# Attention's P times V as two overlapping 128-column products instead of a main product and paired 64-column tails

## What is computed

```python
def _L0_attn_ref(x, W_qkv, b_qkv, W_proj, b_proj):
    b, n, c = x.shape                       # 16, 128, 192
    q, k, v = jnp.split(x @ W_qkv + b_qkv, 3, axis=-1)
    q = q.reshape(b, 8, n, 192)             # likewise k and v
    energy = jnp.einsum('bhqd,bhkd->bhqk', q, k)
    attn = jax.nn.softmax(energy, axis=-1) / 192 ** 0.5
    out = jnp.einsum('bhal,bhlv->bhav', attn, v)
    return out.reshape(b, n, 8 * 192) @ W_proj + b_proj
```

## Time and profile before

| | us |
|---|---|
| median of 3 runs (940.44, 940.95, 943.34) | 940.95 |
| the profiled execution | 939.32 |
| its span, first to last instruction | 937.6 |
| PE busy in the span | 816.1 |
| DVE busy | 526.9 |
| ACT busy | 487.3 |
| attention's P times V, first to last start | 77.8 to 423.6 |
| the next block's first matmul | 433.51 |

### The profile page before, as it was taken

The page is one execution under the profiler, slowest core; times in us unless marked ns, Lnnn a source line. Parts: engine busy times, 40 slices in busy tenths (PEclk is TensorE's granted clock), DMA queues, the critical chain, the costliest instruction groups (busy, mean ns, idle before and its releaser), DMA issues. The chain is left out here.

```text
span 937.6 us, 16696 instructions
## 1 busy us (share of the span) xinstructions
PE 816.1 (87%) x6264; PEld 725.3 (77%) x6264; DVE 526.9 (56%) x1388; ACT 487.3 (52%) x1298; POOL 192.2 (20%) x285
## 2 busy tenths in 40 slices
PE   0599999999999999985685868669989999999997
PEld 0488999999999998974564646558878888898887
DVE  5763645454545454345666656525877556566564
ACT  2255454545353535331566757845645665576653
POOL 4561010202020202021002211200115106042070
PEclk9899999999999999997689989999999999999999
DMA  8433333333333333333001101230000000000000
GB/s 236 115 80 69 77 69 77 69 76 69 77 68 77 69 77 68 77 69 88 1 2 59 61 19 43 60 90 1 1 1 1 1 18 1 1 18 1 17 1 19
DMA packets 33617, 47.34 MB, mean 50 GB/s; under 512 B 4672, under 2 KB 28608, under 8 KB 33536
## 3 DMA queue, kind: packets, MB, share of 16 engines
q1 hardware_dynamic: 28240, 34.63, 16.1%
q0 software_dynamic: 2544, 9.05, 3.4%
q10 hardware_dynamic: 2752, 2.59, 1.1%
HBM read 30.53 MB, written 15.73 MB: 49 GB/s over the span
## 5 line engine op out<-in xcount | busy, mean ns | idle before, releaser
L1488 DVE TENSOR_TENSOR ffn_hid_lo<-ffn_gelu,ffn_hid_hi 128x512 fp32r<-128x512 f32 x120 | 98.0, 818 | 107.2 <-ACT ffn_hid_hi L1462 106.2
L1416 PE MATMUL ffn_ps_out<-ffn_weights_w,ffn_hid_hi 128*128 128x384 f32 x480 | 144.8, 358 | 3.5 <-DVE ffn_hid_lo L1488 3.3
L1458 ACT ACTIVATE ffn_gelu<-ffn_ring,ffn_b 128x512 f32<-128x512 f32 x120 | 82.3, 686 | 113.3 <-PE ffn_ring L1405 111.0
L1417 PE MATMUL ffn_ps_out<-ffn_weights_w,ffn_hid_lo 128*128 128x192 f32 x480 | 121.1, 252 | 0.0
L450 POOL TENSOR_SCALAR attn_probs<-attn_probs,attn_inverse 128x128 f32<-128x128 f32 x128 | 48.2, 376 | 297.2 <-DVE attn_inverse L738 289.5
L1416 PEld LDWEIGHTS ffn_ps_out<-ffn_weights_w,ffn_hid_hi 128*128 128x128 f32 x480 | 90.5, 189 | 9.8 <-DVE ffn_hid_lo L1488 4.9
L1417 PEld LDWEIGHTS ffn_ps_out<-ffn_weights_w,ffn_hid_lo 128*128 128x128 f32 x480 | 91.8, 191 | 4.2
L607 ACT ACTIVATE attn_probs<-ps_scores,attn_neg_max 128x128 f32<-128x128 f32 x128 | 45.3, 366 | 77.6 <-DVE attn_neg_max L734 77.6
L1462 ACT ACTIVATE ffn_hid_hi<-ffn_gelu 128x512 fp32r<-128x512 f32 x120 | 75.9, 633 | 3.8
L1047 ACT ACTIVATE mix_probs<-mix_ps_scores,mix_neg_max 128x128 f32<-128x128 f32 x192 | 67.4, 392 | 17.5 <-DVE mix_neg_max L1145 17.5
L1346 POOL TENSOR_SCALAR ffn_bias_part<-ffn_b,ffn_gates 128x192 f32<-128x192 f32 x64 | 37.4, 600 | 135.8 <-DVE ffn_gates L1522 134.7
(11 more groups left out here) (272 smaller groups left out, 2152.6 us busy)
## 6 DMA issues: line engine op xcount, KB each, us to landing
v_rows<-attn_v_flat SPq DMA_DIRECT2D x16, 768.0 KB, 3.3
attn_v_rows<-v_rows SPq DMA_DIRECT2D x128, 96.0 KB, 3.7
mix_stage<-in_w POOLq DMA_DIRECT2D x5, 576.0 KB, 5.7
mix_stage<-in_w POOLq DMA_DIRECT2D x10, 192.0 KB, 3.4
mix_stage<-in_w POOLq DMA_DIRECT2D x5, 384.0 KB, 4.4
attn_stage_main<-in_w_qkv SPq DMA_DIRECT2D x2, 768.0 KB, 9.0
h_rows<-hin SPq DMA_DIRECT2D x8, 192.0 KB, 2.8
ffn_base<-h_rows SPq DMA_DIRECT2D x1, 1536.0 KB, 9.6
```

Source lines behind the costliest of these rows:

```text
L1416: nc.tensor.matmul(ps_out[:, b, 0:2 * D], hid_hi[:, i % 3, tile], w2[:, c, :, :], start=c == 0, stop=False)
L1417: last = nc.tensor.matmul(ps_out[:, b, 0:D], hid_lo[:, i % 3, tile], w2[:, c, 0, :], start=False, stop=c == HC - 1)
L1458: nc.scalar.activation(gelu[:, i % 2, :], ring[:, bank("L1", i), :], ACT.Gelu, bias=b1[:, f * HC + c:f * HC + c + 1]).then_inc(chunk_read, 1)
L1488: nc.vector.tensor_tensor(hid_lo[:, i % 3, :], gelu[:, i % 2, :], raw(hid_hi[:, i % 3, :]), ALU.subtract).then_inc(lo_ready, 1)
```

## The change

M computes two full products per group: V's dimensions 0 to 127 (side 0) and 64 to 191 (side 1), each 128 columns of weights and 128 streamed columns. Both sides lie in `ps_mixed`, which now has two banks; `ps_pairs` is gone. Dimensions 64 to 127 are computed twice. For even chunks R takes dimensions 64 to 191 from side 1 as a full slice and dimensions 0 to 63 from side 0 on partitions 0 to 63; for odd chunks it takes dimensions 0 to 127 from side 0 and dimensions 128 to 191 from side 1 on partitions 64 to 127. So `mixed_rows` again has twelve slices, eight with one chunk and four with two chunks, and no data changes partition. ACT does side 1 (`take_uppers`: 128x256 and 64x256), DVE side 0 (`take_lowers`: 128x256 and 64x256). The rows of the output weights are laid out accordingly on the host.

```diff
-        ps_mixed = ps("ps_mixed", [P, QUAD, P])
-        ps_pairs = ps("ps_pairs", [P, 512])
+        ps_mixed = ps("ps_mixed", [P, 2, QUAD, P])
...
                 for j, g in enumerate(groups):
-                    nc.tensor.matmul(ps_mixed[:, j, :], v_rows[:, b, g, 0:MAIN], pt[:, n % 2, j, :], start=True, stop=True)
-                for j, g in enumerate(groups):
-                    by_side = pt[:, n % 2, j, :].rearrange("p (c o t) -> p o c t", o=2, t=GROUP)
-                    for odd in range(2):
-                        out = pairs_of(slice(odd * TAIL, (odd + 1) * TAIL))[:, j, :].rearrange("p (c t) -> p c t", t=GROUP)
-                        last = nc.tensor.matmul(out, v_rows[:, b, g, MAIN:D], by_side[:, odd], start=True, stop=True)
+                    for side, cols in enumerate((slice(0, MAIN), slice(TAIL, D))):
+                        last = nc.tensor.matmul(ps_mixed[:, side, j, :], v_rows[:, b, g, cols], pt[:, n % 2, j, :], start=True, stop=True)
                 last.then_inc(mixed.sem, 1)
...
-        def o_place(n, tails):
-
-            at, kinds = (n % (QUADS // UNIT)) * QUAD * GROUP, slice(CHUNKS, KTILES) if tails else slice(0, CHUNKS)
-            return mixed_rows[:, kinds, at:at + QUAD * GROUP].rearrange("p c (j t) -> p j c t", t=GROUP)
+        def o_place(n, part, kinds):
+
+            at = (n % (QUADS // UNIT)) * QUAD * GROUP
+            return mixed_rows[part, kinds, at:at + QUAD * GROUP].rearrange("p c (j t) -> p j c t", t=GROUP)
...
+        def from_mixed(part, side, odd):
+            return ps_mixed[part, side, :, :].rearrange("p j (c o t) -> p j o c t", o=2, t=GROUP)[:, :, odd]
...
-                nc.scalar.activation(o_place(n, False), from_mixed(False), ACT.Copy).then_inc(mains_taken.sem, 1)
+                for part, kinds, odd in ((slice(0, P), slice(0, PAIRS), 0), (slice(TAIL, P), slice(CHUNKS, KTILES), 1)):
+                    last = nc.scalar.activation(o_place(n, part, kinds), from_mixed(part, 1, odd), ACT.Copy)
+                last.then_inc(uppers_taken.sem, 1)
...
-                nc.vector.tensor_copy(o_place(n, True), from_mixed(True)).then_inc(tails_taken.sem, 1)
+                for part, kinds, odd in ((slice(0, P), slice(PAIRS, CHUNKS), 1), (slice(0, TAIL), slice(CHUNKS, KTILES), 0)):
+                    last = nc.vector.tensor_copy(o_place(n, part, kinds), from_mixed(part, 0, odd))
+                last.then_inc(lowers_taken.sem, 1)
...
+    w_even, w_odd = w_proj[0::2], w_proj[1::2]
...
-        "w_proj_main": w_proj[:, :MAIN].transpose(1, 0, 2).reshape(MAIN, QKV),
-        "w_proj_tail": w_proj[:, MAIN:].reshape(CHUNKS // 2, P, D).transpose(1, 0, 2).reshape(P, QKV // 2),
+        "w_proj_main": np.concatenate([w_even[:, TAIL:], w_odd[:, :MAIN]]).transpose(1, 0, 2).reshape(MAIN, QKV),
+        "w_proj_tail": np.concatenate([w_even[:, :TAIL], w_odd[:, MAIN:]], axis=1).transpose(1, 0, 2).reshape(P, QKV // 2),
```

More of the change, by code:

```diff
@@ L307, in attention @@
         mixed = Signal(sem("mixed"), QUADS, lent=QUADS)
-        mains_taken = Signal(sem("mains_taken"), QUADS, lent=1)
-        tails_taken = Signal(sem("tails_taken"), QUADS, lent=1)
+        uppers_taken = Signal(sem("uppers_taken"), QUADS, lent=1)
+        lowers_taken = Signal(sem("lowers_taken"), QUADS, lent=1)
         out_filled = Signal(sem("out_filled"), UNIT, lent=1)
@@ L456, in attention @@
         out_of = lambda b: ps_scores[:, b, :, :].rearrange("p j k -> p (j k)")[:, 0:D]
-        pairs_of = lambda part: ps_pairs[part, 0:QUAD * PAIRS * GROUP].rearrange("p (j k) -> p j k", j=QUAD)
         @block.tensor
@@ L527, in mix @@
                 wait_emptied(pe, turn, source)
-                pe.wait_ge(mains_taken.sem, mains_taken.at(turn, n - 1))
+                pe.wait_ge(uppers_taken.sem, uppers_taken.at(turn, n - 1))
                 apart(pe, keep["passed"])
-                pe.wait_ge(tails_taken.sem, tails_taken.at(turn, n - 1))
+                pe.wait_ge(lowers_taken.sem, lowers_taken.at(turn, n - 1))
                 groups = range(n * QUAD - b * GROUPS, (n + 1) * QUAD - b * GROUPS)
                 for j, g in enumerate(groups):
-                    nc.tensor.matmul(ps_mixed[:, j, :], v_rows[:, b, g, 0:MAIN], pt[:, n % 2, j, :], start=True, stop=True)
-                for j, g in enumerate(groups):
-                    by_side = pt[:, n % 2, j, :].rearrange("p (c o t) -> p o c t", o=2, t=GROUP)
-                    for odd in range(2):
-                        out = pairs_of(slice(odd * TAIL, (odd + 1) * TAIL))[:, j, :].rearrange("p (c t) -> p c t", t=GROUP)
-                        last = nc.tensor.matmul(out, v_rows[:, b, g, MAIN:D], by_side[:, odd], start=True, stop=True)
+                    for side, cols in enumerate((slice(0, MAIN), slice(TAIL, D))):
+                        last = nc.tensor.matmul(ps_mixed[:, side, j, :], v_rows[:, b, g, cols], pt[:, n % 2, j, :], start=True, stop=True)
                 last.then_inc(mixed.sem, 1)
@@ L544, in project_out @@
                 if part == 0:
-                    pe.wait_ge(mains_taken.sem, mains_taken.at(turn, (b + 1) * (QUADS // UNIT) - 1))
-                    pe.wait_ge(tails_taken.sem, tails_taken.at(turn, (b + 1) * (QUADS // UNIT) - 1))
+                    pe.wait_ge(uppers_taken.sem, uppers_taken.at(turn, (b + 1) * (QUADS // UNIT) - 1))
+                    pe.wait_ge(lowers_taken.sem, lowers_taken.at(turn, (b + 1) * (QUADS // UNIT) - 1))
                     if b == 0:
@@ L565, in from_ring @@
             return ring[part, bank(slot), 0:UT].rearrange("p (g t) -> p g t", t=GROUP)
-        def o_place(n, tails):
-            at, kinds = (n % (QUADS // UNIT)) * QUAD * GROUP, slice(CHUNKS, KTILES) if tails else slice(0, CHUNKS)
-            return mixed_rows[:, kinds, at:at + QUAD * GROUP].rearrange("p c (j t) -> p j c t", t=GROUP)
-        def from_mixed(tails):
-            return (pairs_of(slice(0, P)) if tails else ps_mixed[:, :, :]).rearrange("p j (c t) -> p j c t", t=GROUP)
+        def o_place(n, part, kinds):
[3 more added lines that the diff above has]
+            return ps_mixed[part, side, :, :].rearrange("p j (c o t) -> p j o c t", o=2, t=GROUP)[:, :, odd]
         @block.scalar
         def _(act):
-            for signal in (exps_ready, mixed, mains_taken, tails_taken, out_filled, out_read, v_sent):
+            for signal in (exps_ready, mixed, uppers_taken, lowers_taken, out_filled, out_read, v_sent):
                 signal.lend(act)
@@ L614, in turned_probs, with take_uppers @@
                 nc.scalar.activation(pt[:, n % 2, :, :], ring[:, bank(slot), :].rearrange("p (j k) -> p j k", j=QUAD), ACT.Copy).then_inc(emptied["act"].sem, 1)
-            def take_mains(turn, n, slot, hi, source):
+            def take_uppers(turn, n, slot, hi, source):
                 b = n // (QUADS // UNIT)
@@ L633, in _ @@
             weight_his(W_Q)
-            turns({"S": exps, "X": split_x, "T": turned_probs, "Q": take_qk, "R": take_mains, "W": lambda *_: weight_his(W_K)})
+            turns({"S": exps, "X": split_x, "T": turned_probs, "Q": take_qk, "R": take_uppers, "W": lambda *_: weight_his(W_K)})
         @block.vector
@@ L738, in invert, with take_lowers @@
                 nc.vector.reciprocal(inverse[:, n, :], sums[:, n, :]).then_inc(inverse_ready.sem, 1)
-            def take_tails(turn, n, slot, hi, source):
+            def take_lowers(turn, n, slot, hi, source):
                 b = n // (QUADS // UNIT)
@@ L771, in finish @@
                 nc.vector.tensor_tensor(h[:, t, :], out_of(b), h[:, t, :], ALU.add).then_inc(out_read.sem, 1)
-            turns({"A": embed_first, "B": embed_next, "W": query_lows, "N": norm, "S": row_max, "I": invert, "V": biased_v, "X": split_x, "Q": take_qk, "R": take_tails, "F": finish, "Z": mixer_norm})
+            turns({"A": embed_first, "B": embed_next, "W": query_lows, "N": norm, "S": row_max, "I": invert, "V": biased_v, "X": split_x, "Q": take_qk, "R": take_lowers, "F": finish, "Z": mixer_norm})
 def mixer(nc, keep, dram):
```

## The result

The changed kernel takes 944.98 us in the median of six runs (942.02 to 949.07) where the kernel before takes 941.39 beside it (six runs, 940.44 to 943.34): a ratio of 1.0052, 95% interval 1.0029 to 1.0074, so slower by 2.7 to 7.0 us, 4.9 in the middle. The medians alone lie 3.6 us apart, a quotient of 1.0038. Ratios and intervals in this document are worked out from the fast runs alone and are not quotients of the medians beside them; one slow run of the kernel before, of 1983.31 us, is left out of them. The forecast was 954.5, at least 949.0. The sign was right and the size, 13.5 us, about three times too large. A second set of twelve runs gave 944.43 against 941.71, ratio 1.0035 (1.0017 to 1.0053).

The account below looks back on a forecast made before the run. PE was taken to bound the steady turns, a chain through the evacuations the last. 10.4 (matmuls) + 1.0 (ahead of quad 3) + 2.1 (last turn) = 13.5 us on 940.95 gave 954.5 us, range 949.0 to 958.5.

Parts of the forecast that it names:

- What bounds the kernel: Steady turns: PE busy 312.40 of 316.00 us, so in seven of eight turns added PE time adds equally to the total.
- the 0.6 us wait: Every steady turn: a K projection waits 0.60 us for its ring slot until ACT has copied the turned probabilities.
- The matmuls: P times V: new block 1.96 us against 1.59, +0.37 us per quad, 10.4 us in the steady turns.
- the first rival: P times V: the shape change carries a price that goes away with it; not slower, 943 us at break-even; chance 0.05.
- the second: P times V: full products run at the projection's rate, +0.14 a quad, 6.3 us in all, 947 us; chance 0.08.
- no such gap: Trace rows before: they show no gap that would be the array's drain at a change of tiling mode.
- Narrow products cost less together than one full product: P times V: a tail record takes 38 ns against 61, half of a full record's 122.5.
- The evacuations: PSUM copies, each split in two: ACT's pair 0.70 us, +0.10; DVE's pair 0.77 us, +0.35.
- a forecast of 0.15: Steady turns: quad 3 may load at 238.18 instead of 238.03, +0.15 us a turn, 1.0 us over seven.
- The last turn, +2.1 us: Last turn: longer matmuls, evacuation waits and two longer DVE evacuations add 2.1 us, between 1.1 and 2.9.
- forecast 1.45: Last turn: the point where quad 2 is evacuated comes 1.45 us later, including 3 x 0.37 of matmuls.
- The clock: PE's granted clock stays 1.00 in steady turns; behind them work only shifts, with 1 us allowed either way.

Follow-up runs that it names:

- interleaved tails: Kernel before, with each group's two tail products issued right behind its main product, same 24 records per quad: 975.04 us in one run, median beside it 943.00.
- split copies: Kernel before with its matmuls, each engine emptying a quad with two instructions, DVE's second into a spare tile: 939.73 us against 943.00, ratio 0.9989.
- The changed kernel's other profile: The changed kernel once more, unchanged: 944.43 us in twelve runs against 941.71 for the kernel before.
- its further two: Two further profiles of the kernel before, with no edit: 937.83 and 944.06 us in one run each.

## Why the prediction was right and where it failed

**What bounds the kernel** was read rightly. In the steady turns PE's time went into the total one for one, the 0.6 us wait stayed, and the direction came out. For the matmuls it came out by 0.08 us a quad only, a balance in which terms stand that the prediction did not have, so the right sign was in part luck.

**The matmuls, +0.37 us a quad, were the step that failed.** They cost +0.10 in the block and +0.08 in the turn: 2.3 us in place of 10.4. The prediction divided 0.98 us by eight records and took the mean, 122.5 ns, for the price of each. It was seven steps of 112 and one of 205, and the long step belongs to the border with the narrow products, which the change takes away. So the price of the added work was too high (eight more records at about 112, 0.89 us instead of 0.98), and the removed block was counted at 0.61 us, without the parts of its borders that lie in its neighbours' steps, 0.09 ahead and 0.10 behind; it was worth 0.81. Worked out again: before, 7 x 0.112 + 0.205 + 0.613 = 1.60, and 0.10 in the projection's first step, 1.70; after, 1.704 and 0.08 in that step, 1.785, which is sixteen steps of 0.112. What is added is 0.89, what is removed 0.47 of work and 0.34 of borders: +0.08 us a quad, and 28 x 0.08 = 2.2 us.

**The rivals.** The measured +0.08 a quad lies between the first rival's 0 (943 us) and the second's +0.14 (947 us), a run of full products at the projection's rate; they had chances of 0.05 and 0.08. I dismissed the second because "eight in a row show no speeding up": a mean over eight can't show that, and the starts of single records could. The rows for it were there. The projection's records in the earlier trace rows stand between full-sized neighbours on both sides and give 108 ns when scaled; the score mains beside them, called as a second witness for 122.5, have the half-deep tails behind them. The first rival's mechanism, a price for the change of shape, is real (0.34 us a visit between fp32 products of full size, by the interleaved tails), but the narrow products' gain, 0.89 - 0.47 = 0.42 us a quad, is larger still, so the time didn't fall. The Trainium skill says in "TensorEngine Tiling (Array Packing)", Key Properties, that a change of tiling mode drains the engine; these runs agree in that each change costs time, and the prediction's sentence that the rows show no such gap was wrong, since it lay inside the 0.98.

**Narrow products cost less together than one full product**: right, and more so than computed. Two narrow records cost 59 ns, about half of a full record's 112, where the mean of 38 ns a record had made it 76. The full form does cost more per useful column; the removed borders give most of that back.

**The evacuations**: two copies take 0.75 us on DVE (forecast 0.77) and 0.77 on ACT (0.70): ACT's second copy, on partitions 64 to 127, starts 0.40 us after the first and doesn't overlap it, while the two full-height halves of the split copies started 0.28 apart. The profile after, quad 2's copies ahead of quad 3, to be held against the earlier trace rows:

```profile
239.91 0.78 ACT L618 ACTIVATE attn_mixed_rows<-ps_mixed 128x256 f32<-128x256 f32 x2 [4.43 <-PE ps_scores L549]
239.97 0.75 DVE L744 COPY attn_mixed_rows<-ps_mixed 128x256 f32<-128x256 f32 x2 [3.10 <-PE ps_scores L549]
...
240.91 0.19 PEld L534 LDWEIGHTS ps_mixed<-attn_pt,attn_v_rows 128*128 128x128 f32 x1
```

They end at 240.69 and 240.72 and the weights load 0.2 us later. The price is 0.13 us a turn in the mean (335.12 against 334.20, over seven; 0.10 to 0.12 in six turns and 0.26 in one), for a forecast of 0.15. Of the usual 0.11, 0.04 is the later start of quad 3 and 0.07 its longer first step.

**The last turn, +2.1 us**, was read rightly, and is +1.7 as long as the clock stays up. It can be taken up to the start of the second output projection, before any fall of the clock in these two profiles:

```profile
425.96 2.84 PE L553 MATMUL ps_scores<-w_proj_main,attn_mixed_rows 128*128 128x192 f32 x16 [2.14 <-issue]
431.89 4.30 PE L549 MATMUL ps_scores<-w_proj_main,attn_mixed_rows 128*128 128x192 f32 x16 [2.33 <-issue]
```

The first row is before, 16.22 us behind the start of quad 0, and the second after, 17.90 us behind it. The changed kernel's other profile gives 17.90 again, and the kernel before 16.22 in the first of its further two; in the other the clock was low from 410.76 to 417.59. Up to the start of quad 3 the changed kernel needs 13.55 us against 12.34 (quads 0, 1 and 2 begin at 413.99, 417.13, 423.55, quad 3 at 427.54; before at 409.74, 412.44, 418.35, 422.08). In the terms of the prediction: quad 2's evacuation begins 1.03 us later, forecast 1.45, with the 0.37 a quad again too much. DVE's part behind it grew as worked out: from quad 2's copies to quad 3's (the rows below) 4.47 us against 4.15, and 0.33 more from quad 3's copies to the projection.

```profile
426.57 0.75 DVE L744 COPY attn_mixed_rows<-ps_mixed 128x256 f32<-128x256 f32 x2 [1.98 <-PE ps_scores L549]
431.04 0.75 DVE L744 COPY attn_mixed_rows<-ps_mixed 128x256 f32<-128x256 f32 x2
```

The other 1.2 of the 2.9 us between the profiles are the clock: it fell at 433.09, within the projection, whose records then start 320 ns apart in place of 163, and from its start to the last residual add 5.93 us pass instead of 4.73.

**The clock was allowed 1 us either way; that was too little.** The steady turns cost 3.2 us and the last one 1.7, together 4.9, which lies within the measured 2.7 to 7.0 and 1.6 to 5.0. But the second attention, whose code the change doesn't touch, took 187.22 and 185.07 us in the changed kernel's profiles and 183.07 to 183.26 in three of the kernel before. Its mean granted clock goes with it, 0.85 in the longest against 0.87 and 0.88, but not closely: it was 0.87 in the one of 185.07. Over all profiles it was 184.41 to 187.22 us in the four with full products and 181.10 to 184.13 in the seven without. A later start alone does not lengthen it: tails interleaved began it latest, at 469.75, and took 183.82. Whether the change brings this about in another way or these few profiles happened to fall so, stays open; the totals can't tell either, since single runs of one kernel lie up to 8 us apart (937.50 to 945.62 for the kernel before in one set).

## What to carry to other kernels

A mean over a block of equal records is a price only if the block's borders are equal too; look at the starts of single records, and at what stands on either side. Half-width products in pairs are cheap in a long run (59 ns for two records against 112 for a full one) and dear in short visits (0.34 us each between full fp32 products), so put all of them in one visit. By these figures a visit breaks even at 0.34 / 0.053, between six and seven pairs of records (an estimate for this case; visits of two, eight and sixteen pairs are what was measured). Below that full products should be cheaper, which no run here tried. Where the removed work is a visit of its own kind, count what it costs its neighbours.

## What was not expected of the hardware

A change from full to half-depth products has borders of the same kind: from the score mains to the score tails the step is 0.20 us where it is 0.11 in the run. At the border in P times V the weights come late as well:

```profile
221.20 0.19 PEld L533 LDWEIGHTS ps_mixed<-attn_pt,attn_v_rows 128*128 128x128 f32 x1
221.51 0.31 PEld L538 LDWEIGHTS ps_pairs<-attn_pt,attn_v_rows 128*64 128x64 f32 x8
```

The last main record's weights load 0.11 us ahead of it (it starts at 221.31), the first tail's only with it, at 221.51. Whether the products wait for the weights there, or both for the array, no run here separates.

PE's granted clock in the last turn of attention, after idle times of about 2 us, differs from execution to execution of one kernel (1.00, 0.92 and 0.79 over that turn), which moves that turn by up to 3.4 us, as much as the whole change costs in the steady turns.
